# One clearing of the semaphores, behind the first expert stage, in place of six between and behind the groups of stages

## The chip, the cores and the metric

The kernel runs on one core of a Trainium2 chip. A core has five engines with an instruction stream each: TensorE (PE: matmuls, with weight loads shown as PEld), VectorE (DVE), ScalarE (ACT), GpSimd (POOL) and SyncE (SP, which here only issues transfers). The engines agree with each other through semaphores: counters that an instruction raises and another waits for. The metric is device microseconds (us) of one execution; smaller is better.

## The reference

The reference is a small decoder of two layers. `x` has 32 sequences of 56 rows with 128 features, the context 32 sequences of 1500 rows. Each step is `x = layernorm(x + step(x))`:

```python
x = _layernorm(x + _L0_attn_ref(x, ...))            # projection in, a scan with clipped state, gate, projection out
x = _layernorm(x + _L0_xattn_ref(ctx, x, mask, ...))# x attends over 1500 context rows and its own, 2 heads
x = _layernorm(x + _L0_ffn_ref(x, ...))             # 8 experts, the best 2 weighed, relu squared
x = _layernorm(x + _L1_attn_ref(x, ...))            # a Mamba block: convolution, selective scan, gate
x = _layernorm(x + _L1_xattn_ref(x, ctx, ...))      # causal attention over the first 56 context rows, 16 heads
x = _layernorm(x + _L1_ffn_ref(x, ...))             # 8 experts with grouped routing, silu gate
return x
```

Nothing of this arithmetic is touched by the change.

## The kernel before

All of it is one program on one core. `program` (L2666) runs six groups of stages one after the other: `stage_scan`, `stage_attention` (with the first group's projection and norm at its start), `stage_experts0`, `stage_mamba`, `stage_causal`, `stage_experts1`. The activations stay on the chip as `x_tm` (rows by feature) and `xT` (feature by rows). Every group consists of one or several `nc.Block()`s; inside a block each engine has its own hand-written order of work, and at the end of each block all five engines meet: each drains what it has running and adds to a gather semaphore, GpSimd waits for that, and adds to a release semaphore on which the others wait. In the trace these meetings carry the line of their block (L502, L291, L904, L1133, L2359, L1536, L1940, L2186, L2426, L2530, L1773). There are fourteen blocks, since the norms (`stage_norm`, L291) are four blocks of their own; with one meeting at the program's start these are fifteen.

Semaphores come in two sorts. `Core.shared` and the constructor take semaphores that live for the whole program; those of the norms and of the router are counted on from a base and never cleared. `Core.sem` does the same when nothing is lent; but inside `with lent_semaphores(core)` (L101) it takes a plain one and puts it on a list, and at the end of the `with` all engines meet (L106), GpSimd sets the listed semaphores to zero (L107), and all engines meet once more (L108), so that the next group may take the same numbers again and find them at zero:

```python
    core.nc.all_engine_barrier()                       # L106
    core.nc.clear_and_free_semaphores(core.lent)       # L107
    core.nc.all_engine_barrier()                       # L108
```

`program` does this behind each of the six groups: behind `stage_scan`, `stage_attention`, `stage_experts0`, `stage_mamba`, `stage_causal` and `stage_experts1`. So at five places in the middle of the program and at its end the engines meet three times in a row (end of the block, L106, L108). `clear_and_free_semaphores` issues one clear for each run of neighbouring numbers, each with a drain of GpSimd ahead of it. In the program as built these are 16 clears: one of 31 semaphores behind the scan; 9 and 58 behind the attention; 8 and 9 behind the first experts; 7, 9, 4 and 13 behind the Mamba block; 7, 9 and 3 behind the causal attention; 7, 9, 4 and 1 at the end.

Loads that cross such a place: the weights of the experts, of the Mamba block (`load_mamba`, issued in `stage_experts0`) and of the causal attention (`load_causal`, issued in the Mamba block's main loop) have semaphores of their own outside the lists.

Of the kernel before, what the change touches and what calls it, by code (L numbers as in the profile page):

```python
# [25 lines left out]
B, L, D = 32, 56, 128  # L26
T = B * L
# [36 lines left out]
class Core:  # L64
# [8 lines left out]
    def sb(self, name, shape, dt=F32):  # L73
        return self.ctx.enter_context(self.nc.sbuf_tensor(name, shape, dt))

    def sem(self, name):
        if self.lent is None:
            return self.ctx.enter_context(self.nc.semaphore(name))
        self.lent.append(self.nc.alloc_semaphore(name=name))
        return self.lent[-1]  # L80

# [6 lines left out]
@contextmanager  # L88
def scope(core, stage):

    with ExitStack() as ctx:
        def sb(name, shape, dt=F32):
            return ctx.enter_context(core.nc.sbuf_tensor(f"{stage}_{name}", shape, dt))

        def psum(name, shape, dt=F32):
            return ctx.enter_context(core.nc.psum_tensor(f"{stage}_{name}", shape, dt))

        yield sb, psum


@contextmanager  # L101
def lent_semaphores(core):

    core.lent = []
    yield
# [3 lines that stand above are left out]
    core.lent = None  # L109
# [28 lines left out]
def expert_weights(core):  # L138


    core.up, core.down = core.sb("w_up", [D, E, P]), core.sb("w_down", [P, E, D])
    core.route0, core.route1 = core.sb("w_route0", [D, E]), core.sb("w_route1", [D, E])
    core.route_bias = core.sb("w_route_bias", [T2, E])
    core.loaded0, core.loaded1 = core.sem("w_loaded0"), core.sem("w_loaded1")
# [50 lines left out]
def mamba_weights(core, ctx):  # L195

    H2 = INNER // P
    sb, _ = ctx.enter_context(scope(core, "mw"))
    core.mamba = MambaWeights(
        col=sb("col", [P, H2, 12]), alog=sb("alog", [P, H2, DS]), scale=sb("scale", [D, 1]), win=sb("win", [D, 2 * INNER]),  # L200
        wdt_in=sb("wdt_in", [P, H2, MAMBA_R]), wdt_out=sb("wdt_out", [MAMBA_R, INNER]), dtb=sb("dtb", [MAMBA_R, 1]),
        wbc=sb("wbc", [P, H2, P]), bcb=sb("bcb", [P, 1]), wout=sb("wout", [P, H2, D]), bout=sb("bout", [T2, D]),
        xnT=sb("xnT", [D, T]), loaded=core.sem("mw_loaded"))


def load_mamba(core, sp, zeroed):
# [201 lines left out]
def by_batch(xT):  # L408

    return lambda c: (xT[:, c * CH:(c + 1) * CH], lambda ap: ap)  # L410
# [390 lines left out]
def stage_attention(core, gated_projection):  # L801

    nc, d = core.nc, core.dram
    with scope(core, "b") as (sb, psum):
        mk = sb("mk", [D, D])
        mv_ext = sb("mv_ext", [D, HB, VW])  # L810
        qw = sb("qw", [D, B, QR])
        latS = sb("latS", [L, B, HB, L])
        vl = sb("vl", [P, NT, HB, VW])
        aT = sb("aT", [HB * DH, T])
        wout = sb("wout", [HB * DH, D])
        bout = sb("bout", [T2, D])
        negmask = sb("negmask", [P, KT, KP], BF16)
        onehot = sb("onehot", [P, B, QR], BF16)
        xc = sb("xc", [KP, NX0, KT, D])
        loads = [core.sem(f"b_load{x}") for x in range(NX)]  # L820
        stage_latents(core, gated_projection, mk, mv_ext, qw, latS, vl, wout, bout, negmask, onehot, xc, loads)
        with scope(core, "bm") as (sb2, _):
            att = sb2("att", [P, B, DH])
            with scope(core, "bl") as (sb3, psum3):
                stage_context(core, sb3, psum3, mk, mv_ext, qw, latS, vl, att, negmask, onehot, xc, loads)
            heads_to_features(core, "bh", att, aT, None, bout)

        def project(pe, n, out):
            return pe.matmul(out, aT[:, n * T2:(n + 1) * T2], wout[:, :], start=False, stop=True)

        stage_norm(core, "bn", project=project, outT=by_batch(core.xT))
# [1834 lines left out]
def program(nc, dram, out):  # L2666
    with ExitStack() as ctx:
        core = Core(nc, dram, out, ctx)
        stage_constants(core)
        expert_weights(core)  # L2670
        with ExitStack() as gated_scope:
            with lent_semaphores(core):
                gated_projection = stage_scan(core, gated_scope)
            with lent_semaphores(core):
                stage_attention(core, gated_projection)
        with ExitStack() as mamba:
            mamba_weights(core, mamba)
            with lent_semaphores(core):
                stage_experts0(core)
            with ExitStack() as causal:  # L2680
                causal_weights(core, causal)
                with lent_semaphores(core):
                    stage_mamba(core)
                with lent_semaphores(core):
                    stage_causal(core)
        with lent_semaphores(core):
            stage_experts1(core)


# [56 lines left out]
```

## Time and profile before

| | |
|---|---|
| median of three runs | 1257.64 us |
| the three runs | 1234.75, 1257.64, 1258.11 us |
| the profiled execution | 1235.67 us |
| span of its profile, first to last instruction | 1233.9 us |
| mean granted clock of TensorE, of full speed | 0.925 |
| instructions in the trace | 22903 |
| PE / DVE / ACT / POOL busy | 83% / 81% / 58% / 48% of the span |

The busy shares are those of the whole span; TensorE and VectorE carry most stages between them. Meetings, clears and drains are not counted as busy. In the trace's answers a `q` behind an engine's name (SPq, POOLq, PEq) means its instruction queue: meetings are shown there, as `EVENT_SEMAPHORE` and `DRAIN` at the line that made them, and the clears as `EVENT_SEMAPHORE_RANGE_CLEAR`. A wait that is put down to "PEq L108" ended with the meeting of L108.

### The profile page before, as it was taken

The numbers are of one execution on the slowest core, as the hardware profiler recorded it, in microseconds if no ns is written. First come the engines' busy times: TensorE is split into PE (matmuls) and PEld (weight loads), VectorE is DVE, ScalarE is ACT, GpSimd is POOL, SyncE is SP. The second block draws the span as 40 slices with busy tenths as digits, with TensorE's granted clock in tenths as the row PEclk, the third lists the DMA queues.
The fourth block names the chain that finished last, engine by engine and source line by source line (L and its number), as shares of the span: only waits on it lengthen the run. The fifth ranks groups of instructions, "written<-read, shape, count | busy, mean of one in ns | idle before, by whom it ended". The sixth has DMA issues, their size and how long they took to land. (4 is left out here: it accounts for less than half of the span.)

```text
span 1233.9 us, 22903 instructions
## 1 busy us (share of the span) xinstructions
PE 1025.5 (83%) x8317; PEld 747.9 (61%) x8317; DVE 993.4 (81%) x1983; ACT 719.5 (58%) x1522; POOL 594.7 (48%) x899
## 2 busy tenths in 40 slices
PE   5889997476699999999999698690888888768696
PEld 3555653164699999999998566530333333536555
DVE  5989999746699988898886537679999999567575
ACT  3677774055466666666664163275777777147453
POOL 4300000012898888888884141101799999225260
PEclk9899998788899999999999889695899999879989
DMA  3000000020311112111200010002000000000001
GB/s 74 1 1 2 1 2 1 1 107 6 135 51 66 66 74 76 69 67 69 76 2 1 1 24 2 0 1 66 1 0 1 0 1 1 1 1 3 2 1 31
DMA packets 18769, 33.41 MB, mean 27 GB/s; under 512 B 5200, under 2 KB 13888, under 8 KB 18656
## 3 DMA queue, kind: packets, MB, share of 16 engines
q1 hardware_dynamic: 16768, 30.89, 7.3%
q10 hardware_dynamic: 1888, 1.05, 0.4%
q8 instruction: 66, 1.08, 0.4%
q14 instruction: 47, 0.39, 0.1%
HBM read 31.02 MB, written 0.92 MB: 26 GB/s over the span
## 5 line engine op out<-in xcount | busy, mean ns | idle before, releaser
L2256 POOL TENSOR_TENSOR m_h_in<-m_dtu,m_bs 128x448 f32<-128x448 f32 x128 | 144.5, 1148 | 70.4 <-DVE m_dtu L2300 53.6
L774 DVE SCALAR_TENSOR_TENSOR l0r_u<-l0r_u,l0r_a_col 128x1024 f32<-128x1024 f32 x110 | 135.9, 1276 | 6.0 <-ACT l0r_u L684 6.0
L2323 DVE TENSOR_TENSOR_SCAN m_hs<-msp_da,m_h_in 128x448 f32<-128x448 f32 x128 | 136.2, 1081 | 2.4 <-ACT msp_da L2283 1.7
L1155 POOL TENSOR_TENSOR bl_sc<-bl_sc,bl_topall 125x1456 f32<-125x1456 f32 x32 | 105.3, 3290 | 58.3 <-ACT bl_topall L1317 58.3
L684 ACT ACTIVATE l0r_u<-l0r_pu 128x512 f32<-128x512 f32 x216 | 108.4, 642 | 32.3 <-PE l0r_pu L586 32.1
L2219 PE MATMUL msp_py<-m_hc,ident 128*128 128x448 f32 x256 | 118.2, 546 | 0.0
L586 PE MATMUL l0r_pu<-l0r_xs,l0r_eb 32*128 32x256 f32 x896 | 106.4, 460 | 6.9 <-ACT l0r_u L684 4.6
L1392 PE MATMUL bl_pS<-b_qw,bl_xcT 128*125 128x112 f32 x768 | 104.0, 278 | 0.0
L867 POOL MEMSET bq_lT<- 128x256 f32 x1 | 0.3, 312 | 206.6 <-POOLq L108 206.6
L586 PEld LDWEIGHTS l0r_pu<-l0r_xs,l0r_eb 32*128 32x128 f32 x896 | 73.0, 210 | 39.5 <-ACT l0r_u L684 29.0
L2274 ACT ACTIVATE m_bs<-msp_pb 128x448 f32<-128x448 f32 x128 | 69.3, 542 | 45.0 <-PE msp_pb L2203 43.5
L1324 ACT ACTIVATE bl_sq<-bl_pX 125x512 f32<-125x512 f32 x96 | 57.2, 597 | 61.3 <-PE bl_pX L1381 33.0
L1392 PEld LDWEIGHTS bl_pS<-b_qw,bl_xcT 128*125 128x125 f32 x768 | 91.5, 189 | 0.0
L1381 PE MATMUL bl_pX<-b_mk,bl_xcT 128*125 128x128 f32 x768 | 90.1, 274 | 0.0
L1232 DVE TENSOR_REDUCE bl_top<-bl_sc 125x112 f32<-125x1456 f32 x32 | 86.3, 2695 | 1.5 <-DVE bl_sc L1212 0.5
L1381 PEld LDWEIGHTS bl_pX<-b_mk,bl_xcT 128*125 128x125 f32 x768 | 86.9, 189 | 0.2 <-ACT bl_xcT L1262 0.2
L2283 ACT ACTIVATE msp_da<-m_dt,mw_alog 128x440 f32<-128x440 f32 x128 | 80.2, 627 | 5.5 <-DVE m_hs L2323 5.5
L1212 DVE TENSOR_TENSOR bl_sc<-bl_pS,bl_inv 125x448 f32<-125x448 f32 x96 | 59.2, 621 | 27.2 <-PE bl_pS L1392 27.2
L2211 PEld LDWEIGHTS msp_pc<-m_bc,selector 128*128 128x128 bf16 x128 | 12.5, 98 | 102.5 <-DVE m_hc L2309 94.5
L2211 PE MATMUL msp_pc<-m_bc,selector 128*128 128x448 bf16 x128 | 47.6, 372 | 31.8 <-DVE m_hc L2309 31.8
L1246 DVE TENSOR_REDUCE bl_ss<-bl_sq 125x8 f32<-125x512 f32 x96 | 62.8, 682 | 12.9 <-ACT bl_sq L1324 8.8
L779 DVE TENSOR_SCALAR l0r_u<-l0r_u 128x1024 f32<-128x1024 f32 x112 | 72.0, 684 | 0.0
(392 smaller groups left out, 2541.5 us busy)
## 6 DMA issues: line engine op xcount, KB each, us to landing
b_xc<-in_ctx SPq DMA_DIRECT2D x16, 750.0 KB
bl_more<-in_ctx SPq DMA_DIRECT2D x16, 750.0 KB
x_tm<-in_x SPq DMA_DIRECT2D x1, 896.0 KB, 6.6
cw_cT<-in_ctx_headT SPq DMA_DIRECT2D x1, 896.0 KB
out_dram<-x_tm SPq DMA_DIRECT2D x4, 224.0 KB, 2.5
l0r_xr<-in_x ACTq DMA_DIRECT2D x4, 192.0 KB, 5.6
w_up<-in_L_ffn_w SPq DMA_DIRECT2D x1, 512.0 KB, 4.1
w_down<-in_L_ffn_w SPq DMA_DIRECT2D x1, 512.0 KB, 5.3
```

The costliest lines, as they stand in the source:

```text
L586: last = pe.matmul(out, eb[rows, half, j0 + j, :, :], x, start=True, stop=True)
L684: act.activation(u[:, c % RC, :, :, at:at + 2 * B].rearrange("p t r x -> p (t r) x"), pu[:, n % NPU, :].rearrange("p (a x) -> p a x", x=2 ...
L774: ve.scalar_tensor_tensor(state(c, i, r), prev, a_col[:, :], state(c, i, r), ALU.mult, ALU.add).then_inc(s["step"], 1)
L779: ve.tensor_scalar(state(c, i, r), state(c, i, r), 10.0, -10.0, ALU.min, ALU.max).then_inc(s["step"], 1)
L1155: pool.tensor_tensor(sc[0:KP, n % 3, :, :], sc[0:KP, n % 3, :, :], over(topall[0:KP, n % 2, :].unsqueeze(1), [KP, KT + 1, QR]), ALU.subtra ...
L1232: ve.tensor_reduce(top[0:KP, n % 2, :], sc[0:KP, n % 3, :, :].rearrange("p k q -> p q k"), AX, ALU.max).then_inc(s["top"], 1)
L1381: last = pe.matmul(pX[0:KP, u, r * D:(r + 1) * D], xcT[:, n % 2, at], mk[:, :], start=True, stop=True)
L1392: last = pe.matmul(pS[0:KP, u, r * QR:(r + 1) * QR], xcT[:, n % 2, t * KP:(t + 1) * KP], qw[:, n, :], start=False, stop=(r == KS - 1))
L2219: pe.matmul(py[:, g % 2, 0:CH], core.ident[:, :], hc[:, n % NU, :], start=(st == 0), stop=(st == DS - 1)).then_inc(s["summed"], 1)
L2256: pool.tensor_tensor(h_in[:, n % NU, :], dtu[:, half, cols], bs[:, n % NU, :], ALU.mult).then_inc(s["db"], 1)
L2283: act.activation(da[:, n % 2, 0:CH].rearrange("p (b t) -> p b t", t=L)[:, :, 1:L], dt[:, half, cols].rearrange("p (b t) -> p b t", t=L)[:, ...
L2323: ve.tensor_tensor_scan(hs[:, n % NU, :], da[:, n % 2, 0:CH], h_in[:, n % NU, :], 0.0, ALU.mult, ALU.add).then_inc(s["scan"], 1)
```

## The change

Only the places at which semaphores are lent and cleared change. One `with lent_semaphores(core)` now spans the scan, the attention and the first experts, with one clear behind `stage_experts0`. The Mamba block, the causal attention and the last experts run outside of it: their semaphores are plain ones of the program, held until its end and cleared nowhere. The semaphore of the Mamba weights is raised inside the lent part and waited for behind it, so it is taken through a new method, `kept_sem`, that never lends.

```diff
+    def kept_sem(self, name):
+        return self.ctx.enter_context(self.nc.semaphore(name))
+
     def sem(self, name):
         if self.lent is None:
-            return self.ctx.enter_context(self.nc.semaphore(name))
+            return self.kept_sem(name)
...
-        xnT=sb("xnT", [D, T]), loaded=core.sem("mw_loaded"))
+        xnT=sb("xnT", [D, T]), loaded=core.kept_sem("mw_loaded"))
...
-        with ExitStack() as gated_scope:
+        with ExitStack() as mamba:
             with lent_semaphores(core):
-                gated_projection = stage_scan(core, gated_scope)
-            with lent_semaphores(core):
-                stage_attention(core, gated_projection)
-        with ExitStack() as mamba:
-            mamba_weights(core, mamba)
-            with lent_semaphores(core):
+                with ExitStack() as gated_scope:
+                    gated_projection = stage_scan(core, gated_scope)
+                    stage_attention(core, gated_projection)
+                mamba_weights(core, mamba)
                 stage_experts0(core)
             with ExitStack() as causal:
                 causal_weights(core, causal)
-                with lent_semaphores(core):
-                    stage_mamba(core)
-                with lent_semaphores(core):
-                    stage_causal(core)
-        with lent_semaphores(core):
-            stage_experts1(core)
+                stage_mamba(core)
+                stage_causal(core)
+        stage_experts1(core)
```

In the changed file everything below `sem` stands three lines lower, so L108 is L111 there. In the order of instructions GpSimd alone shows a difference, besides the meetings, which that listing leaves out: PE, DVE, ACT and SP have the same rows as before, up to line numbers. On GpSimd the clears stand as `ISA` at L107 (L110 after). Before, behind the last products of the scan's constants (`l0r_cexp`) and ahead of the first memsets of the attention (`bq_lT`):

```order
L549 TENSOR_SCALAR l0r_cexp<-l0r_mine,l0r_cA 128x8 x32
L502 UNCONDITIONAL_BRANCH
L107 ISA
L394 UNCONDITIONAL_BRANCH
L867 MEMSET bq_lT 128x32x8
```

The clear in the middle is gone after the change, and so are those at the three other places and at the end. What stays is on GpSimd behind the squares of the first experts (`f_hidden`), ahead of the Mamba block's scaling of its bias (`mw_bout`); before:

```order
L1693 TENSOR_TENSOR f_hidden<-f_hidden 128x448 x16
L1536 UNCONDITIONAL_BRANCH
L107 ISA x2
L1947 UNCONDITIONAL_BRANCH
L1951 TENSOR_SCALAR mw_bout<-mw_bout 112x128
```

and after:

```order
L1696 TENSOR_TENSOR f_hidden<-f_hidden 128x448 x16
L1539 UNCONDITIONAL_BRANCH
L110 ISA x3
L1950 UNCONDITIONAL_BRANCH
L1954 TENSOR_SCALAR mw_bout<-mw_bout 112x128
```

There two clears have become three. In the program as built they cover 40, 58 and 17 semaphores. In all, 16 clears become 3 and 27 meetings become 17.

## Rows read from the trace of the kernel before

**Rows 1.** The page: TensorE's busy time, and its granted clock in 40 slices.
```profile
PE 1025.5 (83%) x8317; PEld 747.9 (61%) x8317; DVE 993.4 (81%) x1983; ACT 719.5 (58%) x1522; POOL 594.7 (48%) x899
PEclk9899998788899999999999889695899999879989
```

**Rows 2.** Waits of SP's queue: line, releaser, us in total, times, longest.
```profile
SPq L108 <- PEq L108: 5.2, 6, 1.0
SPq L106 <- PEq L106: 1.6, 6, 0.3
```

**Rows 3.** Instructions of L107, whole span: ns min/median/max, first and last start.
```profile
L107 POOLq EVENT_SEMAPHORE_RANGE_CLEAR  x16: 44/78/348, 246.2 to 1233.6; - x16
```

**Rows 4.** Timeline around the five stops in the middle: last work, first work.
```profile
244.83 0.63 DVE L739 TENSOR_TENSOR l0s_gT<-l0r_py,l0r_gate 128x256 f32<-128x256 f32 x1
247.18 0.36 SPq L854 DMA_DIRECT2D bq_lng<-in_L_xattn_ln  x1
...
708.94 0.54 ACT L383 ACTIVATE xT<-bn_xt 128x448 f32<-128x448 f32 x1 [0.95 <-PE bn_xt L306]
711.11 0.15 POOL L1542 MEMSET f0r_earlier<- 112x64 f32 x1 [21.84 <-POOLq L108]
...
794.82 1.14 ACT L1598 ACTIVATE mw_xnT<-f_ph,mw_scale 128x448 f32<-128x448 f32 x2
797.21 0.29 PEld L1962 LDWEIGHTS mip_ps<-mw_xnT,mw_win 128*128 128x128 f32 x1 [3.05 <-issue]
...
1073.06 0.54 ACT L383 ACTIVATE xT<-mn_xt 128x448 f32<-128x448 f32 x1 [1.35 <-PE mn_xt L306]
1075.24 0.11 POOL L2432 MEMSET cl_head<- 128x16 f32 x1 [19.51 <-POOLq L108]
...
1169.70 0.54 ACT L383 ACTIVATE xT<-cn_xt 128x448 f32<-128x448 f32 x1 [0.95 <-PE cn_xt L306]
1171.64 0.15 POOL L1785 MEMSET f_earlier<- 112x64 f32 x1 [19.54 <-POOLq L108]
```

**Rows 5.** Timeline around the end of a block without a clear.
```profile
265.28 1.38 ACT L387 ACTIVATE bq_lT<-l0p_xt,bq_lng 128x448 f32<-128x448 f32 x2
266.93 0.50 PEld L911 LDWEIGHTS bw_ps<-bq_w,bq_lT 128*128 128x128 f32 x2 [2.81 <-issue]
```

**Rows 6.** GpSimd's part in the last block's meeting and in L108, from 1232 us.
```profile
L1773 POOLq EVENT_SEMAPHORE  x2: 17/17/17, 1232.5 to 1232.5; - x2
...
L108 POOLq EVENT_SEMAPHORE  x2: 17/17/17, 1233.8 to 1233.8; - x2
```

**Rows 7.** Clears at 246, 710 and 796 us; GpSimd's drain behind those at 246 and 796.
```profile
L107 POOLq EVENT_SEMAPHORE_RANGE_CLEAR  x1: 203/203/203, 246.2 to 246.2; - x1
L108 POOLq DRAIN  x1: 172/172/172, 246.8 to 246.8; - x1
...
L107 POOLq EVENT_SEMAPHORE_RANGE_CLEAR  x2: 88/218/348, 710.2 to 710.4; - x2
...
L107 POOLq EVENT_SEMAPHORE_RANGE_CLEAR  x2: 69/78/87, 796.6 to 796.8; - x2
L108 POOLq DRAIN  x1: 40/40/40, 796.9 to 796.9; - x1
```

**Rows 8.** Stretches: length, busy PE, PEld, DVE, ACT, POOL; PEclk, DMA share, GB/s.
```profile
707.60:709.60 2.00, 1.01 (x4) 0.66 (x4) 0.24 (x1) 0.94 (x2) 0.00 (x0) 0.50 0.00 0
711.10:715.60 4.50, 4.45 (x24) 4.48 (x25) 0.06 (x1) 1.28 (x1) 0.79 (x4) 0.50 0.30 49
715.60:719.60 4.00, 4.00 (x13) 2.77 (x14) 1.99 (x2) 0.82 (x2) 0.00 (x0) 0.50 0.46 112
725.00:730.00 5.00, 5.00 (x15) 2.58 (x14) 1.88 (x5) 4.82 (x11) 2.85 (x4) 1.00 0.00 0
```

**Rows 9.** Line 1678, the first experts' products: matmul ns min/median/max, first and last start.
```profile
L1678 PE MATMUL f_ph<-xT,w_up x64: 539/539/1094, 717.1 to 750.4; 128*128 128x448 f32 x64
```

## The prediction

> **What bounds the kernel now.** I read the page first, then the waits of SP's queue, then the timeline around every meeting of the engines. The page shows a kernel that is bound by work: TensorE is busy for 1025.5 us and VectorE for 993.4 us of 1233.9 [rows 1]. No stage is touched by this change, so the busy shares can't be what moves. What can move is time in which nothing works. SP has little to do and arrives early at each meeting, so what it waits there, between one release and the next, is the length of the meeting: 5.2 us at the six meetings of L108 and 1.6 us at the six of L106 [rows 2]. That is 6.8 us, 0.55% of the span, for six stops of which one stays; SP's own drains and steps come on top. So the edit is about some 6 us, whatever else is busy.
>
> These stops lie on the path, all of them. The reader is to see in the timeline that at each place the last work of any engine has ended before the stop and the first work of any engine comes behind it: no engine works across one, so there is nothing that hides it. The gap from the end of the last work to the start of the first is 247.18 - 245.46 = 1.72 us behind the scan, 711.11 - 709.48 = 1.63 behind the attention, 797.21 - 795.96 = 1.25 behind the first experts, 1075.24 - 1073.60 = 1.64 behind the Mamba block, 1171.64 - 1170.24 = 1.40 behind the causal attention [rows 4]. The measure for what remains is the end of a block without a clear: 266.93 - 266.66 = 0.27 us [rows 5].
>
> **The change part by part.** *Four stops in the middle go.* Each falls back to a plain end of a block, since the block's own meeting stays: 1.72 - 0.27 = 1.45; 1.63 - 0.27 = 1.36; 1.64 - 0.27 = 1.37; 1.40 - 0.27 = 1.13. Together 5.31 us. Cover is not a question here: nothing runs beside them.
>
> *The stop at the end goes.* GpSimd releases the last block at 1232.5 us and the last meeting at 1233.8, after which only the release lands [rows 6]. The output has been written by then (the last block waits for it), so the span ends 1.3 us earlier. Sum of what goes: 6.6 us. With the 1.25 - 0.27 = 0.98 of the stop that stays it makes 7.6 for all six, of which SP spends 6.8 waiting [rows 2] and the rest in its own drains and steps; the two views agree.
>
> *The stop that stays grows.* It now clears 40, 58 and 17 semaphores where it cleared 8 and 9. The clear behind the scan covers 31 and took 203 ns; the longer one behind the attention covers 58 and took 348; those of 8 and 9 took 69 and 87 [rows 7]. From 31 to 58 that is 5.4 ns for one more semaphore, so I estimate 252 ns for 40 and 127 for 17, and take 348 for 58. Together 0.73 us against 0.16: 0.57 more. A third clear brings a third drain and its step: the stop with three clears at 1171 us is 0.15 longer than that with two at 796 [rows 4], and its shortest clear is under 0.05, so 0.10 more. Then there is a pause that I can't place. The very first clear ended at 246.4 and GpSimd's next drain began only at 246.8 and took 172 ns, where at 796 us the drain followed at once and took 40 [rows 7]: about 0.5 us. If it belongs to the program's first clear it moves to the stop that stays; if it belongs to that place it is gone. I take half, 0.25. The stop grows by 0.57 + 0.10 + 0.25 = 0.9 us, with bounds of 0.67 and 1.2. Nothing hides it either.
>
> *What costs nothing.* Taking other semaphore numbers changes no instruction: every engine waits and raises as often as before, in the same order. Transfers that are issued on one side of a stop and needed on the other start earlier by as much as the rest, since SP stands in the same meetings; with the engines' order unchanged there is nothing for a transfer to collide with that it did not meet before. No stop kept an engine away from a shared port: the ends of the blocks still do that.
>
> *The sum.* 6.6 - 0.9 = 5.7 us. Span 1233.9 - 5.7 = 1228.2; the profiled execution took 1235.67, 1.8 more than its span, which gives 1230.0. The three runs shown are 1234.75, 1257.64 and 1258.11: the profiled execution stands with the lowest, and the median 22 us above it. The change takes the same five stops from either, so from the median it makes 1257.64 - 5.7 = 1251.9, and that is what I predict, since two of the three lie there. It is 0.45% less than the median.
>
> *What TensorE's clock may do with it.* The granted clock was 0.50, the level of 1.2 GHz, already at 707.6 to 709.6 us, where TensorE worked half of the time, and stayed there from 711.1 to 719.6, although TensorE was busy for 8.45 of these 8.5 us; at 725 it was full [rows 8]. So the stage that follows a stop starts slowly, and what I can't read is whether the rise comes with the work or at a time of its own. If with the work, the whole 5.7 us are kept. If the rise stays where it is while the work moves up by the 1.45 + 1.36 = 2.8 us of the two stops ahead of it, there are 2.8 us more at half speed, which do the work of 1.4: half of the gain so far is given back. The same at 1171.6 us, where the work is 2.8 - 0.9 + 1.37 + 1.13 = 4.4 us earlier: up to 2.2 us given back. The Trainium skill has a rule here (TensorE: Matmul & The Clock Gate, Part 1): the hardware's look at TensorE's activity is "free-running" and does not begin with the kernel's work. By that rule a rise would fall anywhere against the moved work, now early and now late; the forecast has it follow on the average.
>
> **The rivals.** *The clock gives half back.* Its place are the entries of the two expert stages, and the price is 1.4 + 2.2 = 3.6 us as worked out above: 5.7 - 3.6 = 2.1 us gained, 1255.5 from the median, 1233.6 from the profiled execution. For it speaks that TensorE is the bound there [rows 8]; against it that the same step can fall early and give as much. Chance 0.13. An early step instead: a gain of 6.6 or more, 1251 or less, chance 0.05.
>
> *The kept stop takes the rest, or the clears were never waited for.* Were the gap at a stop due to something that stays, such as the first instructions of the next block being late, then a plain end of a block would be as long, and it is not: 0.27 against 1.40 to 1.72 [rows 4, 5]. The clears, 16 in the whole span [rows 3], do leave the program but for three, as the order shows. This gives 1257 and is left with 0.04.
>
> *Slower.* One mechanism could do it: TensorE kept at half speed through the first experts' products. One of these 64 matmuls takes 539 ns at full speed and 1094 at half [rows 9]. The loss passes the 5.7 us gained when 5.7 / 0.555 = 10 more of them run at half speed, and with all 64, 35 us, it would be 1257.6 - 5.7 + 35.5 = 1287. For it speaks that the clock does fall between stages, seen as 8 and lower in the slices [rows 1], and that a rise can come late. Against it: the stage holds TensorE at 5.00 of 5 us [rows 8], which is when the clock was granted in full, and a shorter stop leaves TensorE idle for less time ahead of it. Ten matmuls late has a chance of 0.03; over 2% slower (25 us, 56 of the 64) 0.02.
>
> **How the numbers follow.** A gain of 5.4 to 6 us has 0.73, the clock's half 0.13, its early step 0.05, no gain 0.04, slower 0.05. What decides the time in absolute numbers is something else, at which of the two levels of the three runs the next median lies. I split the 0.73 into 0.45 for 1252 and 0.28 for 1230. The likeliest is 1252, with a range of its own of 1251 to 1253. The range that is to hold 8 in 10 must take in both levels: below it the profiled level with the whole gain and some scatter (1234.75 - 5.9 = 1228.9, and 2 us less for scatter), above it the clock's half from the highest run (1258.11 - 2.1 = 1256). I take 1227 to 1256. About 2% is what a measurement of this kernel can tell from no change. The mechanism gives 0.45%, so compared at one level it is within 2% in every case but the last. Faster by over 2% happens when the median before lies at the upper level and the one after at the lower: 1230.0 / 1257.64 is 0.978. The two are measured side by side, so I give that 0.08. Slower by over 2% keeps 0.02, and 0.01 more for what I have not thought of. That leaves 0.89 for the same.
>
> **What would show it right or wrong.** The span of the profile of after should be 1228 us at a granted clock of about 0.92, with three clears in one place near 794 us, of some 250, 350 and 130 ns, and none elsewhere. The gaps behind the scan, the attention, the Mamba block and the causal attention should be 0.27 us. The gap behind the first experts should be 2.2 us (1.25 + 0.9); under 2.0 says that the pause of the first clear stayed behind, over 2.5 that one semaphore costs more than 5.4 ns there. The stretch at half clock behind the attention should begin 2.8 us earlier and be as long as before; if it is longer by 2.8 the clock gave half back. Stages of unequal length inside their blocks, at one clock, would prove me wrong: then semaphore numbers or the place of code matter.

## The result and the profile after

The changed kernel takes 1231.82 us (median of 20 runs, 1225.34 to 1252.5); the kernel before takes 1238.41 us over the 20 runs that it now has (1234.75 to 1258.11). The ratio is 0.9939, interval 0.9918 to 0.9961: 7.6 us, with 4.8 to 10.2 inside the interval. Ratios and means here and below leave out executions that lie over 1.5% above the kernel's fastest; one of before, 1252.81 us, lies just under that bound and is counted, and without it the two means differ by 6.7 us.

The profiled execution took 1227.98 us, its span is 1226.1 us at a granted clock of 0.917, against 1235.67, 1233.9 and 0.925. Its page first, with the rows that answer to [rows 1]: busy time and count of each engine, and the clock in 40 slices.

```profile
span 1226.1 us, 22767 instructions
PE 1023.5 (83%) x8317; PEld 743.5 (61%) x8317; DVE 992.2 (81%) x1983; ACT 719.6 (59%) x1522; POOL 600.8 (49%) x899
PEclk9598989688899999999999979795899999869989
```

The counts of work are those of before; the 136 instructions less are meetings, clears and drains. What SP waits for in the meetings around a clear (against the 5.2 and 1.6 us of [rows 2]), and the instructions of the line that clears (against [rows 3, 7]):

```profile
SPq L111 <- PEq L111: 1.4, 1, 1.4
SPq L109 <- PEq L109: 0.3, 1, 0.3
```

```profile
L110 POOLq DRAIN  x3: 77/103/134, 790.0 to 790.9; - x3
L110 POOLq EVENT_SEMAPHORE_RANGE_CLEAR  x3: 131/248/348, 790.1 to 791.0; - x3
```

Three clears in one place took 248, 348 and 131 ns where 252, 348 and 127 were forecast. The timeline around the same five places as in [rows 4], last work and first work (start, duration, engine and line, what):

```profile
245.81 0.63 DVE L742 TENSOR_TENSOR l0s_gT<-l0r_py,l0r_gate 128x256 f32<-128x256 f32 x1
246.72 0.36 SPq L857 DMA_DIRECT2D bq_lng<-in_L_xattn_ln  x1
...
705.67 0.54 ACT L386 ACTIVATE xT<-bn_xt 128x448 f32<-128x448 f32 x1 [1.35 <-PE bn_xt L309]
706.46 0.40 SPq L222 DMA_DIRECT2D mw_col<-in_L_attn_channels  x1
...
788.26 1.14 ACT L1601 ACTIVATE mw_xnT<-f_ph,mw_scale 128x448 f32<-128x448 f32 x2
791.49 0.50 PEld L1965 LDWEIGHTS mip_ps<-mw_xnT,mw_win 128*128 128x128 f32 x2 [3.89 <-issue]
...
1067.55 0.54 ACT L386 ACTIVATE xT<-mn_xt 128x448 f32<-128x448 f32 x1 [1.35 <-PE mn_xt L309]
1068.34 0.11 POOL L2435 MEMSET cl_head<- 128x16 f32 x1 [18.12 <-POOLq L294]
...
1163.64 0.54 ACT L386 ACTIVATE xT<-cn_xt 128x448 f32<-128x448 f32 x1 [1.20 <-PE cn_xt L309]
1164.43 0.15 POOL L1788 MEMSET f_earlier<- 112x64 f32 x1 [18.39 <-POOLq L294]
```

The gap from the end of the last work to the start of the first is now 0.28, 0.25, 2.09, 0.25 and 0.25 us, where it was 1.72, 1.63, 1.25, 1.64 and 1.40 in the order of the program. At the end GpSimd's last release stands 0.2 us ahead of the span's end, and it is the last block's own; before, that was 1.4 us ahead [rows 6]:

```profile
L1776 POOLq EVENT_SEMAPHORE  x2: 17/17/17, 1225.9 to 1225.9; - x2
```

So the stops give 1.44 + 1.38 + 1.39 + 1.15 + 1.3 = 6.7 us, and the kept one takes 0.84: 5.8 us (forecast 6.6 - 0.9 = 5.7). The two spans differ by 7.8 us. The other 2.0 us lie inside the stages, whose instructions didn't change. I measured each block from its first to its last work in the timelines (us; the last one without the output's transfer):

| block | before | after | before, second profile | after, second profile |
|---|---|---|---|---|
| scan | 244.7 | 245.6 | 245.5 | 243.9 |
| projection and norm ahead of the attention (L0P) | 19.5 | 19.5 | 19.5 | 19.5 |
| attention's weights (BW) | 38.9 | 37.9 | 38.8 | 37.8 |
| attention's loop and heads (two blocks) | 386.2 | 385.9 | 386.2 | 386.4 |
| norm behind the attention (BN) | 16.6 | 15.1 | 16.6 | 15.1 |
| first experts (F0) | 84.8 | 82.9 | 84.9 | 83.3 |
| Mamba block, three blocks | 275.9 | 276.1 | 275.8 | 276.8 |
| causal attention, three blocks | 94.5 | 95.4 | 94.6 | 94.6 |
| last experts (F1) | 58.1 | 58.7 | 58.1 | 58.1 |

BW, BN and F0 gave 1.0 + 1.5 + 1.9 = 4.4 us; the scan, the later stages and rounding took 2.4 back. Where these 4.4 come from is what the experiments below had to find.

The windows of BN and F0, of before and then of after, show the clock beside the length (columns: stretch and length, busy time of PE, PEld, DVE, ACT and POOL with counts; then granted clock, DMA share, GB/s):

```profile
692.88:709.48 16.60, 12.01 (x80) 10.73 (x80) 10.63 (x52) 4.62 (x10) 0.00 (x0) 0.81 0.00 0
711.10:795.96 84.86, 70.92 (x368) 55.35 (x368) 53.65 (x196) 36.45 (x79) 16.40 (x20) 0.84 0.05 9
```

```profile
691.10:706.21 15.11, 10.08 (x80) 8.94 (x80) 10.63 (x52) 4.62 (x10) 0.00 (x0) 0.93 0.00 1
706.50:789.37 82.87, 68.01 (x368) 51.30 (x368) 53.29 (x196) 36.45 (x79) 15.67 (x20) 0.89 0.05 10
```

The same 80 and 368 matmuls kept TensorE busy for 1.9 and 2.9 us less, and VectorE and ScalarE for as long as before: it is TensorE's clock that was granted more, 0.93 against 0.81 and 0.89 against 0.84. The clock has two levels, so a mean of 0.89 says how much of the stretch was at the lower one; such a part is called a half-clock stretch below.

### The profile page after: what moved, and what is told of

The parts are those of the page before. It is cut to its first block and busy times, and to the rows that moved or that the text cites. A ratio compares the mean times of both kernels' runs of the same rounds, so it can differ in the third digit from the quotient of the medians.

```text
span 1226.1 us, 22767 instructions
## 1 busy us (share of the span) xinstructions
PE 1023.5 (83%) x8317; PEld 743.5 (61%) x8317; DVE 992.2 (81%) x1983; ACT 719.6 (59%) x1522; POOL 600.8 (49%) x899
## 5 line engine op out<-in xcount | busy, mean ns | idle before, releaser
L589 PEld LDWEIGHTS l0r_pu<-l0r_xs,l0r_eb 32*128 32x128 f32 x896 | 74.6, 214 | 38.9 <-ACT l0r_u L687 28.2
```

What stands on the lines that cost most here:

```text
L589: last = pe.matmul(out, eb[rows, half, j0 + j, :, :], x, start=True, stop=True)
```

## The experiments

All of them start from the changed kernel but the second profile of before. "Over after" compares means of time with that of after, 1231.0 in the first comparison. Measured again, after had 1227.9 (four executions), so such a difference is known to some 3 us only. What an experiment does to a gap or a stage is read from its profile.

**Is a stop worth its gap?** Two kernels give the stops back many times over, at the five places from which they had been taken. The first adds 8 bare meetings at each, the second four whole stops with a clear of 9 unused semaphores:

```diff
+def extra(core):
+    for _ in range(8):
+        core.nc.all_engine_barrier()
```

> The changed kernel with eight bare meetings of all engines, without a clear, put at each of the five places that lost their stop: 40 meetings. By the trace of before one meeting takes 0.33 us from release to release, so my theory (a stop costs its own length, no more and no less) expects gaps of 0.28 + 8 x 0.33 = 2.9 us at the four middle places, 2.7 us more behind the last block, 13.3 us more than the changed kernel in all: about 7.5 us slower than before less its 7.6 us of gain, so 1.005 of before. The rival (idle time at a stage's entry makes TensorE's clock start later, so a stop costs more than its length) expects the half-clock stretches behind the gaps to grow and more than 18 us. A second rival (part of a stop is hidden) expects less than 10.

```diff
+def extra(core):
+    for i in range(4):
+        core.nc.all_engine_barrier()
+        core.nc.clear_and_free_semaphores([... 9 spare semaphores ...])
+        core.nc.all_engine_barrier()
```

> The changed kernel with four whole stops (meeting, one clear of 9 spare semaphores, meeting) at each of the five places: 20 stops. My theory: 0.33 us for the first meeting, about 0.50 from its release to that of the second with one clear between (0.66 with two clears at 796 us of before, less 0.16 for one clear with its drain), 0.83 us for a stop, 16.6 us in all, 1242.7 us of span and 1.007 of before. If the clears cost more than their rows show, the stop takes over 1 us and the sum is over 20.

The 40 meetings gave a ratio to before of 1.0064 (1.0043 to 1.0085) and a mean of 1245.8 us, 14.8 over after (17.9 over its second mean); the 20 stops 1.0103 (1.0068 to 1.0138) and 1251.3 us, 20.3 over after (23.4). One row of each: where SP waits in the added meetings, and the added clears.

```profile
SPq L2671 <- PEq L2671: 10.6, 39, 0.6
```

```profile
L2672 POOLq EVENT_SEMAPHORE_RANGE_CLEAR  x24: 47/88/92, 247.9 to 1246.6; - x24
```

A meeting takes 0.33 us from release to release. In the first kernel the four gaps in the middle, the kept one and the end grew by 13.9 us together; in the second by 17.4, that is 0.87 a stop. Where the nine spare semaphores lie side by side, a stop takes 0.77 to 0.78 us; behind the Mamba block their numbers lie in two pieces, which is why 20 stops show 24 clears, and a stop takes 0.92 there. Both times nothing was hidden, as forecast (13.3 and 16.6 us), and the program grew by at least 0.9 and 2.9 us more than its gaps. One part of the surplus stands in both: L0P, behind the long gap of 3.4 or 3.9 us, took 22.4 and 22.5 us in place of 19.5. Its window in the kernel with meetings, and in after:

```profile
250.30:272.70 22.40, 15.87 (x112) 15.07 (x112) 11.18 (x57) 11.55 (x30) 1.60 (x2) 0.80 0.29 96
```

```profile
246.70:266.20 19.50, 12.96 (x112) 12.16 (x112) 11.18 (x57) 11.55 (x30) 1.60 (x2) 0.94 0.30 94
```

The same 112 matmuls at a granted clock of 0.80 in place of 0.94 kept TensorE busy for 2.9 us more. In these two profiles a half-clock stretch had begun within the gap and ran 6 us into L0P, which it did in no other. So a gap costs its own length one to one, and may cost more through the clock behind it; whether it does depends on the place. At the attention, gaps of 2.9 and 3.4 us left the first experts at 83.4 and 82.9 us, about as short as in after's two profiles.

**Can the last stop go too?** The kept stop's clears moved into the first experts' block, on GpSimd behind its last squares, where it has nothing else to do. The semaphores cleared are those of the scan and the attention; those of the first experts are then held to the program's end.

```diff
+                core.nc.clear_and_free_semaphores(core.dead)    # GpSimd, in stage_weighed
...
-            with lent_semaphores(core):
+            core.lent = []
...
+            core.dead, core.lent = core.lent, None
```

> The changed kernel without any stop: the semaphores of scan and attention are cleared by GpSimd inside the block of the first experts, behind its squares, where it is idle, and those of the first experts are kept. My theory: the gap behind the first experts falls from 2.09 to 0.27 us, nothing else changes, 1.8 us less than the changed kernel: 0.9924 of before where the changed kernel has 0.9939, which 5 rounds will hardly tell apart, but the profile's gap will. The rival (the clear on a busy core costs its neighbours something) expects the first experts' block to be longer by the clears' 0.7 us or more.

```profile
793.61 1.14 ACT L1602 ACTIVATE mw_xnT<-f_ph,mw_scale 128x448 f32<-128x448 f32 x2
795.02 0.50 PEld L1966 LDWEIGHTS mip_ps<-mw_xnT,mw_win 128*128 128x128 f32 x2 [2.06 <-issue]
```

```profile
L1554 POOLq EVENT_SEMAPHORE_RANGE_CLEAR  x2: 247/298/348, 753.4 to 753.9; - x2
```

The gap is 0.26 us and the clears lie 40 us ahead of it, in GpSimd's free time. The ratio is 0.9936 (0.9916 to 0.9956), against 0.9939 for after: the 1.8 us of the gap don't show beside the scatter of the executions. In the profile they are gone from the gap, but BN took 16.7 and F0 83.6 us here, which is 2.3 more than in after. Up to the end of BN this kernel runs the same program as after, with the same semaphore numbers. That was the first sign that the stages' lengths go their own way.

**Does TensorE's idling in the norms set the half clock behind them?** Three of the norms (BN, that behind the Mamba block and that behind the causal attention) leave TensorE idle while VectorE normalizes. I filled it with matmuls of the identity into an unused corner of the psum tile; nothing reads them.

```diff
+WARM, LAST_WARM = (16, 7), 5
...
+                        if c >= NC and not second:
+                            for _ in range(WARM[c - NC]):
+                                pe.matmul(xt[:, c - 2, 448:512], core.ident[:, :], core.ident[:, 0:64], ...)
...
+                    for _ in range(LAST_WARM):
+                        pe.matmul(xt[:, 0, 448:512], core.ident[:, :], core.ident[:, 0:64], ...)
```

> The changed kernel with matmuls of 128x64 that nobody reads put into TensorE's idle time in the last third of the norms behind the attention, the Mamba block and the causal attention (16, 7 and 5 of them, about 0.1 us each): TensorE's activity is the only thing that changes. If the half-clock stretches at the entries of the expert stages (11.2 and 10.7 us there in the changed kernel, TensorE busy throughout) cost what I say, the clock is full when these stages begin and each is 4 to 5 us shorter: 8 to 11 us less than the changed kernel, span about 1216, 0.986 of before. The rival (the clock's fall does not hang on TensorE being idle there, or these stages are not bound by it) expects no gain, or 1 to 2 us of loss because the added matmuls stand ahead of the transposes.

The ratio is 0.9959 (0.9938 to 0.9979), 2 us slower than after where 8 to 11 us less was forecast. The mechanism is there nevertheless. The router's matmuls at the start of F0 (32 with 8 columns; ns min/median/max), in after and in this kernel:

```profile
L1559 PE MATMUL f0r_pj<-w_route,xT x32: 325/334/334, 706.5 to 712.3; 128*112 128x8 f32 x32
```

```profile
L1566 PE MATMUL f0r_pj<-w_route,xT x32: 235/243/334, 709.8 to 713.3; 128*112 128x8 f32 x32
```

F0 took 80.9 us and F1 56.5, 2.0 and 2.2 less than in after. But the filling was too long:

```profile
702.47 3.70 PE L310 MATMUL bn_xt<-ident 128*128 128x64 f32 x32
706.00 0.55 PE L313 MATMUL bn_xt<-ident,x_tm 112*128 112x112 f32 x4
```

Each added matmul shows as two rows, and 16 of them last 3.70 us, 0.23 each. I had put one at 0.1, so the transposes they stand ahead of came late, at a full clock throughout: BN took 16.8 us, the two others 19.0 and 16.8, 1.7, 1.4 and 1.7 more than in after. With the numbers halved:

```diff
-WARM, LAST_WARM = (16, 7), 5
+WARM, LAST_WARM = (8, 3), 3
```

> The kept-busy kernel with half of the added matmuls (8, 3 and 3), since each took 0.23 us where I had put 0.1, so that they end before the transposes behind them could start. My theory: the three norms are back at 15.1 us where they were 16.8, 15.1 and 17.6 at the others, and the expert stages keep 80.9 and 56.5 us: 4 us less than the changed kernel, 0.990 of before. The rival (fewer of them don't hold the clock up) expects the expert stages at 82.9 and 58.7 again and the changed kernel's time.

The ratio is 0.9934 (0.9911 to 0.9956), mean 1229.4: no better than after beside it, where 4 us less was forecast. F0 took 80.0, the first Mamba block 56.5 and F1 57.3 us, but BN and the norm behind the causal attention 16.2 and 16.4. It isn't the short filling that delays them. In both a half-clock stretch lay over the first 3 to 4 us, where nothing was added, and with such a stretch these norms take 16.7 us without any filling (in the kernel without a stop). When the short filling was profiled once more, in the last experiment below, BN had no such stretch and took 14.7 us, the shortest of all. BN of this kernel and of that one (columns as above):

```profile
692.80:709.00 16.20, 14.20 (x108) 13.41 (x108) 10.63 (x52) 4.60 (x10) 0.00 (x0) 0.90 0.00 1
```

```profile
694.80:709.50 14.70, 12.63 (x108) 11.90 (x108) 10.63 (x52) 4.62 (x10) 0.00 (x0) 1.00 0.00 1
```

What was won behind the norms here was lost where half-clock stretches fell otherwise, in the norms and in the attention's loop, which took 380.5 us where it had 378.3 in after. That these losses are the filling's isn't shown.

**Do the differences repeat?** The two kernels as they are, once more:

> The changed kernel itself once more. My theory (the change takes 5.8 us of stops and nothing else; what the first comparison showed beyond that is scatter of TensorE's clock) expects 5.8 us less than before, 0.9953, within the scatter, and stages whose lengths differ from those of the first profile of the same kernel by as much as the two kernels' did: the norm behind the attention at 15.1 or 16.6 us, the first experts anywhere from 82 to 85. The rival (other semaphore numbers or the shorter code save 2 us more) expects 0.9938 and the same stage lengths again.

> The kernel before once more, for a second profile of the same code. My theory expects the gaps at the stops as before to 0.05 us (1.72, 1.63, 1.25, 1.63, 1.39), with the pause behind the scan's clear there again, and stages that differ from the first profile by 1 to 2 us where a half-clock stretch falls otherwise. If the stages are equal to those of the first profile to 0.1 us, the 2 us are the change's.

After again: ratio 0.992 (0.9898 to 0.9942), which is 9.9 us, median 1228.73, profile 1226.34 us with a span of 1224.4. Before again, in one execution: 1236.34 us with a span of 1234.6 at a clock of 0.908. The table above has both beside the first profiles. Of before every block but the scan came back within 0.1 us, though the mean clock was 0.908 in the one and 0.925 in the other; BW, BN and F0 differ between before and after by the same 1.0, 1.5 and 1.6 to 1.9 us in both pairs. What varies between two profiles of one kernel is the scan, by 0.8 and 1.7 us, and in after some other blocks by up to 1.2.

Two pairs are few, and the other profiles serve as more. Up to the end of BN the kernel without a stop and that with the attention's stop (below) run after's own program. BW took 37.7 us in both, so its 1.0 holds. BN took 16.7 in both, as in before, so its 1.5 us do not belong to the kernels. And their attention's loop took 380.6 us where after's two profiles have 378.3 and 379.1, without one instruction changed. The loop in after and in the kernel without a stop:

```profile
304.60:682.90 378.30, 359.76 (x3296) 350.27 (x3296) 320.32 (x768) 238.80 (x577) 295.74 (x616) 0.99 0.17 61
```

```profile
305.20:685.78 380.58, 362.75 (x3296) 353.19 (x3296) 320.17 (x768) 239.07 (x577) 297.23 (x616) 0.98 0.17 61
```

**Both additions together**, clears under the first experts and the short filling:

> No stop at all and the half set of added matmuls in the norms, together. The two act at different places, so my theory adds them: 1.8 and 4 us less than the changed kernel, 0.989 of before. The rival (the clock's gain is not there) expects 0.993, that of no stop alone.

The ratio is 0.9895 (0.9875 to 0.9915), mean 1224.8 us, 13 less than before. Its F0 (columns as above):

```profile
710.40:789.70 79.30, 64.56 (x368) 48.31 (x368) 53.84 (x196) 36.51 (x79) 16.59 (x20) 0.93 0.05 10
```

**Is it the place of the stops in time, or the semaphores' numbers?** Three kernels. One gives the scan's group its own stop back, and keeps that behind the first experts:

```diff
-            with lent_semaphores(core):
-                with ExitStack() as gated_scope:
+            with ExitStack() as gated_scope:
+                with lent_semaphores(core):
                     gated_projection = stage_scan(core, gated_scope)
-                    stage_attention(core, gated_projection)
-                mamba_weights(core, mamba)
-                stage_experts0(core)
+                core.lent = []
+                stage_attention(core, gated_projection)
+            mamba_weights(core, mamba)
+            stage_experts0(core)
+            core.nc.all_engine_barrier()
+            core.nc.clear_and_free_semaphores(core.lent)
+            core.nc.all_engine_barrier()
+            core.lent = None
```

> The changed kernel with one of its edits undone: the stop behind the scan is back, with its clear of 31 semaphores; the rest is as changed. Both profiles of the kernel before have the block behind the first norm (weights of the cross-attention) at 38.8 to 38.9 us, the changed kernel's two at 37.8 and 37.9. Theory of the clock's place (the end of the scan stands in a fixed relation to the clock's steps, so the length of the gap behind it settles where a rise falls in the next stages): gap 1.7 us, that block at 38.9 again, 2.5 us slower than the changed kernel in all. Theory of the numbers or the code (other semaphore numbers, less code): the block stays at 37.8, 1.4 us slower.

One gives back the stop behind the attention, by a `with lent_semaphores` around the scan and the attention and another around the first experts:

```diff
-                mamba_weights(core, mamba)
+            mamba_weights(core, mamba)
+            with lent_semaphores(core):
                 stage_experts0(core)
```

> The changed kernel with the stop behind the attention back and nothing else; the clears of scan and attention (two, of 40 and 58 semaphores) happen there, that behind the first experts has one clear. Gaps of about 2.0 behind the attention and 1.1 behind the first experts where the changed kernel has 0.25 and 2.07: 0.8 us more. The first experts took 84.8 and 84.9 us before and 82.9 and 83.3 after. Theory of the clock's place: with the stage starting 1.7 us later against the clock's steps it takes another length, 84.9 if the stop is what made it slow. Theory of the numbers: it stays at 83.

One adds two bare meetings behind the scan, and so keeps every number:

```diff
                     gated_projection = stage_scan(core, gated_scope)
+                    for _ in range(2):
+                        core.nc.all_engine_barrier()
```

> The changed kernel with two bare meetings behind the scan: a gap of 1.0 to 1.3 us there, between the 0.28 of after and the 1.72 of before, no semaphore number and no clear changed. Theory of the clock's place: the block behind the first norm takes neither 37.8 by necessity nor 38.9; the clock rises in it at another distance from its start than the 4.0 us of the changed kernel's profile, and its length moves by 0.3 us or more. Theory of the numbers: 37.8 to 0.1 us.

The ratios are 0.9955 (0.9938 to 0.9971), 0.9934 (0.9911 to 0.9956) and 0.9939 (0.9919 to 0.9959). BW in each, in this order:

```profile
267.70:305.40 37.70, 29.41 (x213) 18.07 (x213) 19.94 (x38) 21.04 (x51) 7.58 (x4) 0.86 0.09 37
```

for the scan's stop, and

```profile
265.60:302.80 37.20, 28.98 (x213) 17.97 (x213) 19.93 (x38) 21.02 (x51) 7.58 (x4) 0.87 0.11 44
```

for the two meetings; 37.7 also with the attention's stop. F0 with the scan's stop, the attention's stop and the two meetings:

```profile
711.50:795.10 83.60, 69.25 (x368) 53.06 (x368) 53.76 (x196) 36.54 (x79) 15.72 (x20) 0.87 0.05 9
```

```profile
712.60:797.40 84.80, 70.91 (x368) 55.34 (x368) 53.63 (x196) 36.37 (x79) 16.44 (x20) 0.84 0.05 9
```

```profile
707.70:790.70 83.00, 68.01 (x368) 51.32 (x368) 53.35 (x196) 36.55 (x79) 15.73 (x20) 0.89 0.05 10
```

With the attention's stop F0 is back at 84.8 us and 0.84, as in both profiles of before, and as forecast from the clock's place. This edit changes two things, the time and the semaphore numbers of F0, so it has to be read beside the kernel without a stop: the same program up to the end of BN (16.7 us in both), then 0.25 us of gap where this one has 1.78. F0 began 1.5 us later against the half-clock stretch at its entry and took 84.8 us in place of 83.6. In all profiles but those of the filled kernels and of the two with 40 meetings and 20 stops, the place of that stretch orders F0's length. It ended 8.9 us behind F0's start in the three with 84.8 to 84.9 us, 10.3 in the two with 83.6, 10.7 in that with 83.3, and 11.2 and 11.3 in those with 82.9 and 83.0. The two with 83.6, no stop and the scan's stop, have different semaphore numbers in F0, and the same length.

BW follows the clock in the same way. The half-clock stretch that begins in L0P ended 5.9 and 5.7 us into BW in before, 4.1 and 3.9 in after, 3.6 with the scan's stop and 2.9 with the two meetings, and BW took 38.9, 38.8, 37.9, 37.8, 37.7 and 37.2 us. That stretch in before and with the two meetings:

```profile
262.60:272.80 10.20, 6.85 (x14) 4.02 (x15) 1.54 (x11) 6.07 (x18) 0.00 (x0) 0.50 0.32 133
```

```profile
261.60:268.40 6.80, 3.81 (x9) 2.28 (x10) 1.18 (x10) 4.26 (x11) 0.00 (x0) 0.50 0.33 134
```

Two meetings alone, with all numbers the same, made the gap behind the scan 1.0 us longer than in after's second profile; the stretch ended 1.0 us nearer to BW's start, and BW took 0.6 us less. So time between the blocks is enough to move a stage's length. The forecast for BW failed, though: the scan's own stop did not bring back the 38.9 us, L0P took the loss instead (21.1 us, granted clock 0.85 from 246.0 to 267.4). That kernel gives the attention the numbers that it had in before, so the numbers aren't what made BW long. Its mean is 1.4 us over after, or 4.5 over after's second, for a gap 1.4 longer. Why the stretch was 10.2 us long in before and 6.8 in every other kernel isn't shown, so BW's 1.0 us is traced to the clock, but not to one edit.

**The best version once more**, as it had the lowest ratio:

> The kernel without any stop and with the half set of added matmuls once more, the fastest so far at 0.9895 of before. If that was its own, the ratio is again 0.988 to 0.991 and below the changed kernel's 0.9939 and 0.992; if it was scatter, it comes back at 0.993.

0.9901 (0.9881 to 0.9921), mean 1225.6, where the two kernels measured beside it that lie next to after have 0.9934 and 0.9939. Taken with 0.9895 before, it is faster than before by about 1%, and its mean lies 2 to 6 us under any mean of after. Its interval meets those of after, 0.9918 to 0.9961 and 0.9898 to 0.9942, so that it beats after is likely rather than settled; each of its two halves alone was not told from after. F0 took 82.0 us this time, where the same kernel had 79.3:

```profile
709.80:791.80 82.00, 67.40 (x368) 51.49 (x368) 53.80 (x196) 36.41 (x79) 16.00 (x20) 0.88 0.05 10
```

## Why the prediction was wrong, point by point

**The failed step is the level.** "Two of the three lie there" is what the prediction said of 1257.64 and 1258.11 when it took the median as the time to subtract from. Three runs did not carry that: of 20, four lie at 1252 or above, and the median is 1238.41. Against that the forecast of 1252 is not a gain at all. Taken from the new median the same sum is 1238.4 - 5.7 = 1232.7, against 1231.82 measured. The sum from the profiled execution, 1230.0, was 1.8 off. The profiled execution, 1235.67, was nearer to the kernel's usual time, and the text had seen that it stood with the lowest run; the chances were split 0.45 to 0.28 the wrong way round. Two of three neighbouring executions at one level were taken as a share of two thirds; the share is one fifth of those 20, and over all 71 executions of before on record, 7 took 1250 us or more. That both fell among the first three was bad luck; to build on three was the mistake. What makes such an execution isn't known from these runs.

**The mechanism held, for the part that it covers.** The stops had no cover, as read from [rows 4]: each gap fell to 0.25 to 0.28 (forecast 0.27), the end lost its 1.3 us, and the 40 meetings and 20 stops came back in the time at least one to one. The gaps in the trace gave 5.8 us where 5.7 were forecast. As a time, 5.7 us is 0.9954 of 1238.4, inside the first measured interval but outside the second, which ends at 0.9942. The span came out at 1226.1 where 1228 was forecast. What is over lies inside the stages and was put at nothing.

**The kept stop.** 2.09 us measured, 2.15 by the sum. The clears cost what 5.4 ns a semaphore gave, to 4 ns. The term that was mis-sized is the pause, half of 0.5 us: it did not come along. The three clears and their drains follow each other without a pause at 790 us, and the growth is 0.84, of which 0.57 is the clears' longer run. The rest is 0.27, put at 0.10: the three drains took 134, 103 and 77 ns, 0.17 more than the two of 70 before, and steps make up the rest. Of two terms one was 0.17 too small and one 0.25 too large. That the sum was so near is in part luck. The pause needs no clear. With two bare meetings behind the scan, the gap was 1.30 us, 1.02 over a plain end, where two meetings cost 0.66 by the 0.33 above:

```profile
243.90 0.63 DVE L742 TENSOR_TENSOR l0s_gT<-l0r_py,l0r_gate 128x256 f32<-128x256 f32 x1
...
245.83 0.31 POOL L870 MEMSET bq_lT<- 128x256 f32 x1 [202.96 <-POOLq L2679]
```

GpSimd had been without work for 203 us there. Whether this is why stays open: no run changed it, and among the 20 added stops a second pause of this kind stands close to the program's end, behind a clear that ended at 1245.5 us and ahead of a drain that began at 1245.8 and took 182 ns. The threshold given for it, a gap under 2.0, was not reached, and it was badly chosen: it had no room for the drains.

**The clock.** I left it at nothing, with two rivals of opposite sign. What happened at F0's entry is what the rival "the clock gives half back" described, seen in the stretch of half clock (before, then after; half-clock stretch of 13.7 us in both):

```profile
706.30:720.00 13.70, 10.87 (x44) 8.80 (x45) 3.92 (x9) 3.19 (x5) 0.79 (x4) 0.50 0.24 49
```

```profile
704.00:717.70 13.70, 12.20 (x43) 9.15 (x44) 5.29 (x7) 4.34 (x8) 1.72 (x5) 0.50 0.24 52
```

As forecast it was as long as before, and began 2.3 us earlier (forecast 2.8). But the work had moved up by 4.6 us by then (stops 2.8, stages the rest), so F0 ran for 11.2 us at half clock after its entry, where it had been 8.9. By the prediction's own rule that gives 1.15 us back. It was more than made up further on: before had half-clock stretches of 6.8, 6.8 and 4.3 us in F0's last 30 us, after two of 3.4. At the last experts' entry the stretch ended 1.5 us deeper in the work than before and F1 took 0.6 us longer, against 2.2 at most in the forecast; after's second profile does not have this. The first two of before's late stretches in F0, then the first of after's:

```profile
767.80:774.60 6.80, 6.19 (x29) 6.20 (x30) 4.78 (x19) 0.00 (x0) 0.00 (x0) 0.50 0.01 2
781.40:788.20 6.80, 6.09 (x29) 6.09 (x30) 5.02 (x20) 0.00 (x0) 0.00 (x0) 0.50 0.00 0
```

```profile
765.50:768.90 3.40, 3.40 (x19) 3.40 (x18) 2.09 (x9) 0.00 (x0) 0.00 (x0) 0.50 0.02 5
```

The prediction quoted a rule here, that the hardware's look at activity is "free-running" (the Trainium skill, TensorE: Matmul & The Clock Gate, Part 1). The traces agree in part: rises and falls stand at other places of the work when the work moves, as with the two meetings. But they did not fall anywhere. In before's two profiles the stretch at F0's entry lay at the same place of the work to 0.03 us, and that in L0P to 0.2, though the scans ahead differed by 0.8 us. What the forecast added, that this would cancel on the average, was the weak part. It does not have to cancel in one program: F0 fell badly in both profiles of before and with the attention's stop, and better by 1.2 to 2 us in all other kernels without filling; BW fell better by some 1.0 us or more in every kernel but before. BN fell better in after's two profiles, and badly again in two kernels with the same program up to there. Nor need it be a gain: the loop had 378 us in before and 380.6 in those two.

**"Stages of unequal length inside their blocks, at one clock, would prove me wrong."** They are unequal, but not at one clock, so semaphore numbers or the place of code are not needed. The scan's stop, which gave BW and BN their old numbers back and left BW at 37.7 us, speaks against the numbers. The place of code was not changed by itself in any run.

**The chances.** Within 2% had 0.89 and came; the range of 1227 to 1256 holds both the median and the profile. Its width was there for the wrong reason, the two levels, and that it holds the result is luck.

## What to carry to other kernels

Read a stop of all engines from the gap between the last and the first work of any engine; where nothing crosses it, its removal is worth that gap, 0.33 us a meeting here, and a clear is 5.4 ns a semaphore on top. When a change is worth half a per cent, first ask from how many executions the time before is known: three can have their median at a level that one in five has, or one in ten. Then compare each stage's length beside its granted clock, since work that only moves in time can gain or lose 1 to 3 us a stage without a single instruction having changed. Two profiles that agree are not enough to give such a gain to a kernel: look for a third kernel that runs the same program up to that stage.

## What the runs showed of the hardware

A meeting of five engines costs 0.33 us when nothing runs, a stop with one clear of 9 semaphores 0.77 to 0.78. Clears of 9, 17, 31, 40 and 58 semaphores took 88, 131, 203, 248 and 348 ns, with a GpSimd drain of 0.06 to 0.13 us ahead of each where it had nothing running. Small ones do not go by 5.4 ns a semaphore: in before, clears of 1, 3 and 4 took 44 to 47 ns, of 7 and 8 68 to 69, of 9 87 to 88, and of 13 109. That looks like steps of 20 to 22 ns for four semaphores each.

TensorE's mean clock over a span told little of the time: before was profiled at 0.925 and at 0.908 and took 1235.67 and 1236.34 us, while after at 0.917 took 1227.98. Which stage has the half clock decides; in before it was the scan that had 0.94 in one profile and 0.85 in the other, with 244.7 and 245.5 us. The attention's loop follows TensorE's clock too, though its mean hardly shows it (0.99, 0.98 and 0.98): in after, in before and in the kernel without a stop the same 3296 matmuls were busy for 359.8, 360.1 and 362.8 us, and the loop took 378.3, 378.4 and 380.6.

At F0's entry TensorE was busy for 6.09 of 6.10 us at a granted clock of 0.50, with matmuls of 8 columns:

```profile
706.50:712.60 6.10, 6.09 (x33) 6.10 (x33) 0.06 (x1) 1.26 (x1) 0.76 (x4) 0.50 0.35 88
```

and a matmul of 64 fp32 columns with its weights took 0.23 us at full clock, so that filling an idle TensorE without making it late takes an exact count: 16 made BN 1.7 us longer, 8 did not.
